# Attention and gated-FFN block on one core: the uses of one PSUM bank moved by one step within a batch, and at most three weight pieces a batch on GpSimd

## What is computed

```
x = x + _layernorm(_L0_attn_ref(_layernorm(x, axis=-1), W_qkv, b_qkv, W_out, b_out, rel_bias), axis=-1)
x = x + _layernorm(_L0_ffn_ref(_layernorm(x, axis=-1), w1_w, w1_s, w2_w, w2_s, h1_w, ..., w3_s), axis=-1)

# attention: scores = q k^T / sqrt(8) + bias[i - j]; softmax; times v; times W_out, plus b_out
# ffn: h = silu(x w1) * (x w2); h = gelu(h h1); h = gelu(h h2); h w3   (each scaled by its own vector)
```

## Time and profile before

| | us |
|---|---|
| timed runs | 314.26, 307.68, 313.43 (median 313.43) |
| profiled execution, its own time | 308.98 |
| its span | 307.1 |
| TensorE busy | 272.3 (89%) |
| VectorE busy | 215.7 (70%) |
| ScalarE busy | 196.8 (64%) |
| GpSimd busy | 94.8 (31%) |

### The profile page before, as it was taken

One profiled execution on the slowest core, in us unless ns is written; L12 is line 12 of the kernel. 1 busy time (PEld: TensorE's weight loads), 2 busy tenths in 40 slices (PEclk: granted clock), 3 DMA queues, 4 the chain that ended last, 5 costly groups with the idle time before them and its releaser, 6 DMA issues.

```text
span 307.1 us, 5106 instructions
## 1 busy us (share of the span) xinstructions
PE 272.3 (89%) x1864; PEld 181.2 (59%) x1864; DVE 215.7 (70%) x440; ACT 196.8 (64%) x291; POOL 94.8 (31%) x98
## 2 busy tenths in 40 slices
PE   8886499999999999999998799876899999999980
PEld 8663254545555455465554355434687888888860
DVE  3847263888978988989987779872753855474575
ACT  2531244868678688685774776955548978696750
POOL 3110210010250510751996981012851200410111
PEclk9999555999999999999999799999999999999996
DMA  6879910352322044454221200000000000010012
GB/s 161 280 215 254 296 63 2 95 184 61 99 72 84 24 115 163 176 139 140 62 73 44 73 1 1 3 2 1 0 0 3 0 0 0 2 34 0 2 35 73
DMA packets 22747, 23.29 MB, mean 76 GB/s; under 512 B 3744, under 2 KB 19904, under 8 KB 22464
## 3 DMA queue, kind: packets, MB, share of 16 engines
q1 hardware_dynamic: 21872, 22.38, 25.1%
q10 hardware_dynamic: 848, 0.54, 0.7%
HBM read 15.93 MB, written 6.68 MB: 74 GB/s over the span
## 4 chain that ended last, share of the span: by engine, by line
PE 49%; DVE 19%; ACT 9%; POOL 8%; DMA 7%; issue 6%; SPq 1%; ACTq 0%; POOLq 0%; DVEq 0%
PE place L1374 9%; PE place L1375 9%; PE place L1194 7%; PE pv L1244 6%; DVE mx L672 6%; ACT ring L960 4%; PE place L1220 4%; PE place L1184 3%; DMA raw<-ext 3%; DVE stats L598 2%; DVE y_and_z L609 2%; POOL w_hi L558 2%; DMA k_first<-z_parts 2%; POOL w_lo L550 2%; POOL xn L560 2%
## 5 line engine op out<-in xcount | busy, mean ns | idle before, releaser
L672 DVE TENSOR_REDUCE mx<-place 128x4 f32<-128x1024 f32 x64 | 78.0, 1222 | 26.9 <-PE place L1194 25.7
L960 ACT ACTIVATE ring<-place 128x1024 f32<-128x1024 f32 x64 | 65.6, 1027 | 9.3 <-PE place L1231 4.5
L509 POOL TENSOR_TENSOR rstd<-mv,mhalf 128x2 f32<-128x2 f32 (+1 forms) x26 | 20.9, 805 | 155.6 <-DVE mv L606 155.6
L1194 PE MATMUL place<-room,identr 128*128 128x512 f32 x128 | 49.7, 471 | 6.0 <-ACT room L926 3.6
L967 ACT COPY place<-raw 128x1024 f32<-128x1024 f32 x37 | 37.8, 1020 | 21.6 <-DVE mx L672 21.6
L1374 PE MATMUL place<-room,w_hi 128*128 128x512 f32 (+1 forms) x116 | 44.6, 387 | 0.7 <-DVE room L792 0.7
L1375 PE MATMUL place<-room,w_hi 128*128 128x512 f32 (+1 forms) x116 | 44.1, 382 | 0.0
L1244 PE MATMUL pv<-ring,vx 128*9 128x256 f32 x512 | 35.3, 395 | 2.4 <-ACT ring L960 2.4
L792 DVE TENSOR_TENSOR room<-ring,room 128x512 fp32r<-128x512 f32 x32 | 21.4, 689 | 18.6 <-ACT room L1051 18.6
L1184 PE MATMUL place<-room 33*128 33x256 f32 x256 | 29.6, 309 | 5.2 <-ACT ring L960 2.4
L1220 PE MATMUL place<-room 33*128 33x256 f32 x256 | 33.3, 341 | 0.8 <-DVE place L679 0.5
(11 more groups left out here) (131 smaller groups left out, 412.2 us busy)
## 6 DMA issues: line engine op xcount, KB each, us to landing
raw<-ext SPq DMA_DIRECT2D x8, 384.0 KB, 5.9
room<-q_parts SPq DMA_DIRECT2D x48, 64.0 KB
room<-k_parts SPq DMA_DIRECT2D x48, 64.0 KB
w_lo<-h SPq DMA_DIRECT2D x2, 1024.0 KB, 5.8
q_parts<-w_hi SPq DMA_DIRECT2D x4, 256.0 KB, 3.2
k_parts<-w_hi SPq DMA_DIRECT2D x2, 512.0 KB, 3.5
xs<-x SPq DMA_DIRECT2D x3, 256.0 KB, 6.4
w_lo<-w SPq DMA_DIRECT2D x3, 256.0 KB, 2.7
```

The lines of the kernel that those rows point to most:

```text
L509: nc.gpsimd.tensor_tensor(rstd[:, at:at + width], mv[:, at:at + width, 1], mhalf[:, 0:width], ALU.pow).then_inc(rstd_set, 1)
L672: nc.vector.tensor_reduce(mx[:, s // RPAIRS, :, :, s % RPAIRS].rearrange("p i k -> p k i"), max_tile(b * PAIRS + s)[:, :, :].rearrange("p ...
L960: nc.scalar.activation(probs[:, s % PRING, :, :, :].rearrange("p k j n -> p (k j n)"), score_tile(b * PAIRS + s)[:, :, :].rearrange("p k n ...
L1194: last = mm(max_tile(b * PAIRS + s)[:, half, :], identr[:, :], windows(table_hi[:, 2 * s + half, :], 0, P, 2, S), start=False, stop=True, ...
```

## The change

Every use of the small bank moves one step later, except that `norm_T`, `keep_zT` and `z_low` move from step 7 to the first step of the next batch, with the index of the batch adapted. `maxima_T(b, 1)` with its `minus_max` goes from step 0 to step 1 (batch 0 keeps it in step 0), the two `back` to steps 2 and 3, `heads_T` to 4, `project` to 5, `maxima_T(b + 1, 0)` to 6. The x work goes from step 6 to step 7, and there it stands between `scores` and `max_scores` instead of behind `weighted`. In the last batch the transpose of `w_low_top` goes from step 4 to step 6, behind `weighted`. On GpSimd one piece of weights moves from batch 4 to batch 5 and one from batch 5 to batch 6. The line numbers of the changed file are three higher on TensorE.

```diff
-        SPLIT_AT = ((), (0,), (1,), (2, 3), (4, 5, 6, 7), (8, 9, 10), (), ())
+        SPLIT_AT = ((), (0,), (1,), (2, 3), (4, 5, 6), (7, 8, 9), (10,), ())
...
                     if b > 0:
-                        if s in (1, 2):
-                            weigh(b - 1, s - 1)
-                        if s == 3 and b + 1 == B:
+                        if s == 0 and b > 1:
+                            z_low(b - 2)
+                        if s in (2, 3):
+                            weigh(b - 1, s - 2)
+                        if s == 4 and b + 1 == B:
                             largest_low()
-                        if s == 4:
+                        if s == 5:
                             attn_moments(b - 1)
+                        if s == 6:
                             if b + 1 == B:
                                 any_low()
-                        if s == 5:
                             residual(b - 1)
-                        if s == 6:
+                        if s == 7:
                             second_norm(b - 1)
...
-                        if s == 7 and b + 1 < B:
-                            z_low(b - 1)
...
                     if s == 0:
+                        if b > 1:
+                            keep_zT(b - 2)
                         if b > 0:
                             keep_weighted(b - 1, GROUPS - 1)
-                        minus_max(b, 1)
...
+                    elif s == 1:
+                        minus_max(b, 1)
-                    if s == 3 and b > 0:
+                    if s == 4 and b > 0:
                         keep_onT(b - 1)
-                    if s == 5 and b + 1 < B:
+                    if s == 6 and b + 1 < B:
                         minus_max(b + 1, 0)
...
                     scores(b, s)
+                    if s == 7 and 1 <= b <= 4:
+                        pe.wait_ge(mrow_set, b * RANGES + 3)
+                        if b == 1:
+                            x_T(4)
...
+                        if b in (2, 3):
+                            q_and_k(4, b - 2)
+                        if b == 4:
+                            v(4)
```

More of the change, by code:

```diff
@@ L991, in _ @@
                     if s == 0:
+                        if b == 2:
+                            for u in range(0, 3):
+                                act.wait_ge(parts_out[u], PARTS_OUT)
+                        if b > 1:
+                            keep_zT(b - 2)
                         if b > 0:
                             keep_weighted(b - 1, GROUPS - 1)
-                        minus_max(b, 1)
-                        if b == 0:
+                    if b == 0:
+                        if s == 0:
+                            minus_max(b, 1)
                             send_mrow(act, 0, 1)
-                    if b == 0:
                         if s == 1:
@@ L1012, in _ @@
                             q_and_k_high(4, b - 2)
-                    if s == 7 and b > 0 and b + 1 < B:
-                        if b == 1:
-                            for u in range(3):
-                                act.wait_ge(parts_out[u], PARTS_OUT)
-                        keep_zT(b - 1)
             keep_weighted(B - 1, GROUPS - 1)
@@ L1301, in _ @@
                     if s == 0:
+                        if b > 1:
+                            if b == 2:
+                                pe.wait_ge(xT_set, 5)
+                            elif b in (3, 4):
+                                pe.wait_ge(qk_lo_set, 6 + b)
+                            elif b == 5:
+                                pe.wait_ge(v_set, 5)
+                            else:
+                                pe.wait_ge(mrow_set, b * RANGES + 1)
+                            norm_T(b - 2)
                         if b > 0:
                             weighted(b - 1, GROUPS - 1)
-                        if b > 1:
-                            pe.wait_ge(z_lo_set, b - 1)
                         if b == 0:
                             pe.wait_ge(mrow_set, 1)
-                        maxima_T(b, 1)
-                    else:
-                        if s % 2 == 0:
-                            weighted(b, s // 2 - 1)
+                            maxima_T(b, 1)
+                    elif s % 2 == 0:
+                        weighted(b, s // 2 - 1)
                     if b > 0:
                         if s == 1:
+                            if b == 1:
+                                pe.wait_ge(mrow_set, 3)
+                            else:
+                                pe.wait_ge(z_lo_set, b - 1)
+                            maxima_T(b, 1)
+                        if s == 2:
                             pe.wait_ge(mrow_set, b * RANGES + 2)
                             back(b - 1, 0)
-                        if s == 2:
+                        if s == 3:
                             back(b - 1, 1)
-                        if s == 3:
+                        if s == 4:
                             heads_T(b - 1)
-                        if s == 4:
+                        if s == 5:
                             if b == 1:
@@ L1323, in _ @@
                             project(b - 1)
-                            if not more:
-                                pe.wait_ge(y_read, b)
-                                pe.wait_ge(w_low_top_set, 2)
-                                mm(misc[0:1, 0:P], w_low_top[:, :], ident[:, :], start=True,
-                                   stop=True).then_inc(w_low_row, 1)
-                    if b == 0:
+                        if s == 6 and not more:
+                            pe.wait_ge(y_read, b)
+                            pe.wait_ge(w_low_top_set, 2)
+                            mm(misc[0:1, 0:P], w_low_top[:, :], ident[:, :], start=True,
+                               stop=True).then_inc(w_low_row, 1)
+                    else:
                         if s == 1:
@@ L1341, in _ @@
                             v(3)
-                    if s == 6 and 1 <= b <= 4:
-                        pe.wait_ge(mrow_set, b * RANGES + 3)
-                        if b == 1:
-                            x_T(4)
-                        if b == 2:
-                            pe.wait_ge(xT_set, 5)
-                        if b in (2, 3):
-                            q_and_k(4, b - 2)
-                        if b == 4:
-                            v(4)
-                    if s == 5 and more:
+                    if s == 6 and more:
                         if b == 0:
@@ L1357, in _ @@
                         maxima_T(b + 1, 0)
-                    if s == 7 and b > 0 and more:
-                        if b == 1:
-                            pe.wait_ge(xT_set, 5)
-                        elif b in (2, 3):
-                            pe.wait_ge(qk_lo_set, 7 + b)
-                        elif b == 4:
-                            pe.wait_ge(v_set, 5)
-                        else:
-                            pe.wait_ge(mrow_set, b * RANGES + 3)
-                        norm_T(b - 1)
             weighted(B - 1, GROUPS - 1)
```

3 lines of the change are left out of this document (added).

## The result

The changed kernel takes 317.29 us (median of four executions, 312.26 to 324.74), the kernel before 311.38 on the same chip. The ratio is 1.0164 with a 95% interval of 1.0084 to 1.0245. So it is slower, by 1.6% where 1.2% was forecast; between the medians it is 5.9 us, where 3.8 were forecast. A ratio here leaves disturbed executions out, so it need not be the quotient of two medians. The profiled execution of the changed kernel has a time of its own of 318.09 and a span of 316.2, and it holds falls of the granted clock.

A forecast was written before the change was run, and what follows sets the result against it. TensorE and VectorE were both taken as nearly full, so the wait that ends last counts. Gains, mainly -4.4, and costs summed to +3.8 us, put on the mean of 311.1: 315 us, range 306 to 322.

The forecast's parts named there:

- What the order does to a batch: Whole attention batches: batches 2 to 4 should take about 22 us, batch 5 about 21.
- The weigh in the chain: Steps 3 to 6: VectorE's second weigh enters the 6.44 us chain of maxima, 0.63 us in six batches, +3.8.
- norm_T out of the shadow: Batch boundary: norm_T (0.36 us) no longer lies within the wait for step 7's exponent but follows it; +1.8.
- Its new wait, and that for z_low: Batch start: norm_T waits for second_norm and q_and_k_low, +1.2; maxima_T waits for z_low in step 1, +1.5.
- The maxima's way back: Step 7's x work waits for ScalarE's copy, +1.2; DMA rows land 2.4 us after issue, +0.3 for batch 0.
- The table: Three GpSimd pieces instead of four end batch 5's 3.34 us stop, gaining 2.8, plus 1.6 of clock: -4.4.
- The last batch: It starts about 1.4 us later but loses a 0.80 stop before the w_low_top transpose; +0.6.
- The clock of batch 6: Batch 6's granted clock, 0.92 before, should stay full: a gain of 1.6 us.
- more is late than I count: Rival: rows' DMA takes 3.8 us and GpSimd holds second_norm; about 322, either alone about 318; chance 0.20.
- Only the stop: Rival: small waits trade one for one, leaving -4.4 from batch 5's end, perhaps less; 307; chance 0.19.

The follow-up runs named there:

- e2_order_only: Changed kernel with the old table of weight pieces (four in batch 4, three in batch 5), so only the new order; 314.59 us.
- e7_after_w2: Changed kernel with one weighted product (group 2) moved from step 6 to behind the next batch's first scores; 316.10 us.
- e1_split_only: Kernel before with only the table of weight pieces changed to three a batch; 305.47 us, ratio 0.9888.
- e5_after_zwait: Changed kernel with GpSimd waiting for second_norm (z_set) before its weight pieces; 310.59 us, ratio 1.0043.
- e12_after_4_in_5: Changed kernel with piece 10 moved back from batch 6 to batch 5, making four pieces there; 320.11 us, ratio 1.0305.
- e3_after_short_weigh: Changed kernel with the second weigh of batches 1 to 5 cut to two single-column reciprocals; 317.69 us, ratio 1.0294.
- e4_before_short_weigh: Kernel before with the second weigh of batches 1 to 5 cut to two single-column reciprocals; ratio 1.0109.
- e10_split_again: Repeat of e1_split_only: kernel before with three weight pieces a batch; 304.47 us, ratio 0.9864.
- e11_split_zwait_again: Repeat of e6_split_zwait: kernel before with three pieces a batch and GpSimd's wait for second_norm; 304.95 us, ratio 0.9891.
- e8_split_zwait_w2: e6_split_zwait with one weighted product (group 2) moved from step 6 to behind the next batch's first scores; ratio 0.9890.
- e6_split_zwait: e1_split_only with GpSimd waiting for second_norm (z_set) before its weight pieces; 304.99 us, ratio 0.9880.

## Why the prediction was right, point by point

The direction holds, and so does the mechanism within a batch. The size is in part luck: +3.8 us were forecast, the medians are 5.9 apart and the two spans 9.1. Of the 9.1, by estimate, 4.0 (batch 4) and 2.1 (last batch) are falls of the granted clock, for which the sum has no term. Without them +3.0 is left against the forecast +3.8. Some terms are wrong and cancel.

- *What the order does to a batch.* Confirmed. Forecast: batches 2 to 4 at about 22 us, batch 5 at about 21; measured 22.15, 22.14, 22.59 (in `e2_order_only`, at full clock) and 20.81. With batch 4 at 22.59, batches 1 to 6 come to 0.69 + 1.23 + 1.31 + 1.82 - 1.76 - 0.32 = +3.0 us; the terms of the sum without batch 0 and the last batch gave +2.9.
- *The weigh in the chain: 0.63 us, 3.8 in all.* Right in mechanism, as the two short weighs show, and too large: I added duration and gap of each instruction, but the next one starts before the last has ended. It is 0.49, 2.9 in all.
- *norm_T out of the shadow.* Confirmed: 2.29 to 2.31 us from bias to `max_scores` in all batches, with an empty 0.77 in it at the ends of batches 1 to 4, and `norm_T` behind it. `e7_after_w2` gets a product into it.
- *Its new wait, and that for z_low.* Too large: 1.2 and 1.5 us were forecast over the batches, and the waits measure 0.6 (0.17, 0.18 and 0.27) and 0.33. Still, from the start of a batch to the chain the six batches take 1.05 us more, where these two, `norm_T` and the `back` that left made +0.9 (batch 4 read in `e2_order_only`, batch 6 against `e1_split_only`). So the `back` that left gave less than the 0.6 that it was taken for: batch 1, which has no `norm_T`, is 0.41 shorter there. Two errors cancel, which is luck.
- *The maxima's way back.* 0.3 a batch with x work, and 2.4 us from issue to use: measured 0.62 us more from `max_scores` of step 6 to the bias of step 7 in batch 2, of which `maxima_T` is 0.31 and the later start of the x work 0.18; and 2.35. Over the six batches that stretch grows by 3.0, and with `maxima_T`'s 0.3 a batch 3.0 were forecast. I had this only for the first half of the rows. The second half's rows stand behind `load_rows` in batch 4, and their wait of 0.81 (+0.4 on the batch) is a term that the sum lacks.
- *The table: -4.4.* Here the step fails. It is true of the old order alone, where `e1_split_only` gets 1.1 to 1.4%. I took the stop as a cost that the table removes, and did not look what the move of `residual` by a step does to it by itself: it hides all but 0.76 us of GpSimd's lateness. The two parts of the change remove the same stop; it was counted once, so the sum survives, but most of it was put down to the wrong part. The table brought 0.8 us in batch 6, and its price, piece 10 beside the last `second_norm`, is 1.1 us of wait and what the clock adds.
- *The last batch: +0.6.* Measured +2.1. With `e2_order_only`'s 15.52 and 1.14 us more of wait it would by estimate be 16.66 at full clock, as long as before; the 2.1 are the clock. The sentence that failed is that piece 10 is done long before its result is asked for: true, but the piece slows `second_norm` from 0.60 to 1.73 us, and this batch has no maximum after it that would cover a wait. `e5_after_zwait` shows it: with the piece held back the wait is 0.46.
- *The clock of batch 6: -1.6.* It came back, and fell elsewhere. The sum had a gain for the stop removed and no price for the waits added. In the profiled execution, batch 4 loses 26.57 - 22.59 = 4.0 us by it, and the last batch some 2.1.

Of the rivals, "more is late than I count" came nearest to what happened in the profiled execution, by a held `second_norm`, though at another place and through the clock, not the DMA. "Only the stop" is `e1_split_only`, and it describes what the order gave away.

What stays open is the fall in batch 4. TensorE's timeline there, changed kernel, and a window of the stretch:

```profile
132.75 0.44 PE L1278 MATMUL misc<-ident,y_and_z 128*128 128x128 f32 x2 [0.18 <-DVE w_hi L629]
133.12 1.81 PE L1247 MATMUL pv<-ring,vx 128*9 128x256 f32 x16
```

```profile
133.10:143.20 10.10, 10.10 (x63) 5.18 (x64) 5.04 (x7) 5.88 (x9) 5.72 (x5) 0.51 0.51 170
```

The clock goes to half (the 1.2 GHz level) behind waits of 0.77 and 0.18 us, where batch 3 has the same two and stays at 1.00. `e12_after_4_in_5` fell at the same place (chain of steps 3 to 6 at 9.42 us, batch at 28.97), and `e2_order_only` and `e3_after_short_weigh` with the same two waits did not, in their profiled executions; nor did `e5_after_zwait`, which has the 0.77 alone, and `e7_after_w2`, which has 0.40 at `norm_T` alone. No run tells what decides it.

## What to carry to other kernels

When a use is moved off a step, write down two things for it: what it waited for, and whose wait it lay in; leaving a shadow costs its full length, and entering a chain between two instructions costs it too. Before a second edit is credited with removing a stop, ask what the first does to the same stop, since two cures for one wait do not add. Background work on GpSimd should be placed by what VectorE does beside it as well as by when its result is due, and a stop on TensorE counts for more than its length wherever the clock falls behind it, which a sum made at full clock leaves out.

## What the runs showed of the hardware

- *The clock behind a stop.* In attention, behind the start, every profiled stop of TensorE of 1.60 (changed kernel), 1.65, 1.70, 2.99 and 3.30 to 3.34 us was followed by a granted clock of 0.50 for a while: some 3 us in the kernel before, 7 in the changed kernel, 13 in `e4_before_short_weigh` and 16 in `e3_after_short_weigh`. Stops of 1.04 to 1.10 us (`e1_split_only`, `e2_order_only`, `e10_split_again`) were not. The length of the stop alone does not decide, though. At the start of the feed-forward part twelve of the fourteen profiled executions stop for 1.73 to 1.75 us and none of them falls behind it; the changed kernel, in the first line below, is at 1.00 from there to 226 us. And the clock also fell behind waits under 0.9 us. What decides is open. The second line is the window behind the stop in `e4_before_short_weigh`, which shares it with the kernel before:

```profile
221.53 0.50 PE L1381 MATMUL place<-z_parts,w_hi 128*128 128x512 f32 x1 [1.73 <-DVE ring L805]
```

```profile
171.18:185.00 13.82, 13.82 (x80) 7.46 (x79) 5.94 (x10) 7.65 (x10) 10.94 (x10) 0.53 0.08 21
```

- *Spread.* The mean clock of an execution was under 0.940 in 8 of 56 executions of the eight experiments without a profiled stop of 1.6 us in attention, in 25 of 54 of the kernel before that ran beside the experiments, and in 18 of 22 of the changed kernel and the four experiments with such a stop (`e3`, `e4`, `e7` and `e12`). So such stops go with low clocks, but neither is needed for the other: the 8 are three of ten of `e5_after_zwait`, two of four of `e2_order_only`, two of six of `e11_split_zwait_again` and one of eight of `e10_split_again`. The profiled execution of `e11_split_zwait_again` is at 0.65 and 0.50 from 200 to 210 behind waits of 0.80 and 0.88 us only, and `e8_split_zwait_w2`, with the same two waits, at 0.50 from 201 to 210.5; `e6_split_zwait` has them too and stays at 1.00. The profiled execution of `e10_split_again` (0.936) loses it ahead of batch 2, in a longer low stretch of the start, so the mean clock alone does not tell where a fall lies.
- *VectorE beside GpSimd.* A pair of scale-and-shift instructions on 128x128 takes 0.59 to 0.60 us alone and 1.55 to 1.83 beside a piece of weights (and 0.89 beside a memset and a cast, in batch 1 of the kernel before), while a maximum out of PSUM takes 1.22 or 1.23 in either case. The Trainium skill, GPSIMD Engine Reference (section "Specifications"), says that GpSimd's SBUF interfaces are shared with VectorE and contend with some of its instructions; by the wait on `z_set`, which takes `second_norm` back to 0.59, this case agrees.
- *A small transfer.* Two DMAs of 4 KB inside SBUF let the waiting matmul start 2.35 us after the first issue, in three places (175.74 to 178.09 above, 139.38 to 141.73 and 172.15 to 174.50 in `e2_order_only`). The Trainium skill, DMA: Bandwidth & Descriptors (section "Anatomy of one DMA"), has some 2.0 us of fixed cost, for a DMA that GpSimd issues. With the 0.60 us of one issue before it that is an estimate of 2.6 us for these two of SyncE, and the measured 2.35 decides.
